# Second expert mixture: half 1's rows scattered by plain transfers, and all shared tiles placed behind the routed ones

## The chip, the cores and the metric

The kernel runs on one core of a Trainium2 chip. The core has a matrix engine (TensorE, called PE in the profile), a vector engine (DVE), a scalar engine (ACT), a general-purpose engine (POOL) and a sequencer for transfers (SP). SP and POOL issue the transfers of this kernel (DMA); 16 DMA engines carry them out. The metric is the device time of one execution in microseconds (us). Faster and slower are told from no change at 0.3%, about 3.7 us here.

## The reference, cut to what matters

Four layers follow each other: attention, a first mixture of experts, a state-space layer, and a second mixture of experts. Only the second mixture is changed:

```python
def _L1_ffn_ref(x, gate_w, gate_b, w1, b1, w3, b3, w2, b2, sw1, sb1, sw3, sb3, sw2, sb2):
    D, H, E, K = 128, 176, 8, 2
    xf = x.reshape(-1, D)                       # 4096 tokens
    scores = jax.nn.softmax(xf @ gate_w.T, axis=-1)
    _, idx = lax.top_k(scores + gate_b, K)      # two experts of eight for each token
    w = jnp.take_along_axis(scores, idx, axis=-1)
    rw = zeros((T, E)).at[arange(T)[:, None], idx].add(w)
    h = silu((einsum('td,edh->teh', xf, w1) + b1) * (einsum('td,edh->teh', xf, w3) + b3))
    oe = einsum('teh,ehd->ted', h, w2) + b2
    y = einsum('te,ted->td', rw, oe)            # the routed experts
    z = _expert(xf, sw1, sb1, sw3, sb3, sw2, sb2)   # the shared expert, for every token
    return (y + z).reshape(shape)
```

## The kernel before

The 4096 tokens are 32 tiles of 128 rows, in two halves of 16 tiles: half 0 (tiles 0 to 15) and half 1 (tiles 16 to 31). In a mixture each half is routed by itself. Each of its tokens is written twice, once for each of its two experts, into a table in device memory (`rows1`, in the code `XG`), at a slot in which the rows of one expert stand together. The table is filled with zeros long before. One write of 128 rows is a **scatter** (`pool_scatter`, line 858): one indirect transfer that POOL issues, with the slots as its index. Half 1 has 32 of them, 16 for the first choice and 16 for the second; between the two passes POOL waits until the first 16 have landed and puts the second weight into the rows (`pool_reweight`, line 852). The argument `op` says whether a scatter adds to what stands in the table (`ALU.add`) or writes over it (`ALU.bypass`).

The **routed tiles** are blocks of 128 rows of that table: 39 for each half (`NH`), 78 in all (`NT`). A routed tile is fetched by SP (line 1074), turned, sent through the expert's two layers by PE, ACT and DVE, weighted, and stored by SP into another table, `out_rows1` (line 1079). The **shared tiles** are the 32 tiles of tokens themselves, fetched by SP from on-chip memory (line 1069). All 110 tiles go through one software pipeline, in the order of the list `sequence`. Each engine walks the list; at step s, SP fetches tile s and stores tile s - 8 (`LAG`), PE turns tile s - 3, and DVE puts out tile s - 6. The fetch of a routed tile waits until its half has been scattered (`placed`), and every fetch waits until the tile four places ahead of it has been turned. SP runs its list in order, so what stands behind a waiting fetch waits as well.

When all routed tiles of a half are stored, POOL **gathers** (line 1131): 32 indirect transfers that add the rows of `out_rows1` to the tokens `X`, 16 for each choice, the second 16 after the first have landed. POOL runs in one order: the scatters of half 1, the gathers of half 0, the gathers of half 1.

The shared tiles of half 0 are added to `X` as they come out (lines 1320 and 1324), after half 0's gathers. Those of half 1 are put into a buffer of their own, `late` (line 1309), and are added to `X` at the very end, four tiles at a time, as soon as half 1's gathers for these tiles have landed (line 1371). SP then writes the output (line 1096).

The stages around the change, in the order of time: the state-space layer (its POOL work is line 1900), the function `dispatch`, which scatters half 0 and routes half 1, and `experts`, called with `inside=False` for the second mixture. The first mixture calls the same `experts` with `inside=True` and no shared tiles. In the names of the profile `m_x_G` is a fetched tile, `m_x_UP`, `m_x_HP` and `m_x_DP` are the matrix engine's outputs, `m_x_YO` a finished tile and `g_X` the tokens.

Of the kernel before, what the change touches and what calls it, by code (L numbers as in the profile page):

```python
# [12 lines left out]
ALU = mybir.AluOpType  # L13
# [5 lines left out]
T = B * S // P  # L19
# [4 lines left out]
HT = T // 2  # L24
NH = 2 * HT + E - 1
NT = 2 * NH
# [898 lines left out]
def experts(nc, tag, signals, d, inside, X, rt, XG, Y, out, n_early, w, gated, ident, ahead=None):  # L925
# [7 lines left out]
    n_shared, scale_col, H = w.n_shared, w.ns, w.H  # L933
# [6 lines left out]
    LAG = 8  # L940
    R = 4 * U

    sequence = [(False, i) for i in range(NH)]
    if n_shared:
        sequence += [(True, i) for i in range(HT, HT + LAG)]
    sequence += [(False, i) for i in range(NH, NT)]
    if n_shared:
        sequence += [(True, i) for i in range(HT)] + [(True, i) for i in range(HT + LAG, T)]
    place_of_shared = {i: j for j, (shared, i) in enumerate(sequence) if shared}

    def stores(v, through):
# [3 lines left out]
    def stores_of(v, end):  # L955

        return sum(1 for j, (shared, i) in enumerate(sequence) if not shared and i < end and j % U == v)
# [27 lines left out]
    with ExitStack() as ctx:  # L985
# [51 lines left out]
        with nc.Block() as block:  # L1037
# [62 lines left out]
            @block.gpsimd  # L1100
            def _(pool):
                if inside:
                    d.pool_scatter(pool, 1, HT // 4, HT, ALU.bypass)
                pool.wait_ge(d.s.sent.sem, d.s.sent.after(0))
                pool.sem_inc(placed, NH)
                for k in range(2):
                    d.pool_reweight(pool, 1, k)
                    d.pool_scatter(pool, k, HT, T, ALU.add)
                pool.wait_ge(d.s.sent.sem, d.s.sent.after(1))
                if inside:  # L1110
                    pool.wait_ge(d.s.tabled.sem, d.s.tabled.after(1))
                pool.sem_inc(placed, NH)
                if out is None:

                    for v in range(U):
                        pool.wait_ge(stored[v], 16 * stores_of(v, NH))
                    for k in range(2):
                        for t in range(n_early):
                            nc.gpsimd.indirect_dma_start(X[:, t * D:(t + 1) * D], None, Y[0:NH * P, :],  # L1119
                                                         bass.IndirectOffsetOnAxis(rt.slot[k][:, t:t + 1], 0),  # L1120
                                                         compute_op=ALU.add).then_inc(early, 16)
                        pool.wait_ge(early, 16 * n_early * (k + 1))
                else:
                    for h in range(2):
                        for v in range(U):
                            pool.wait_ge(stored[v], 16 * stores_of(v, (h + 1) * NH))
                        for k in range(2):
                            if k == 1:
                                pool.wait_ge(joined, 16 * HT * (h + 1))
                            for t in range(h * HT, (h + 1) * HT):  # L1130
                                nc.gpsimd.indirect_dma_start(X[:, t * D:(t + 1) * D], None, Y[0:(h + 1) * NH * P, :],  # L1131
                                                             bass.IndirectOffsetOnAxis(rt.slot[k][:, t:t + 1], 0),
                                                             compute_op=ALU.add).then_inc(got[t % HT // W] if k else joined, 16)
# [70 lines left out]
            def _(act):  # L1204
# [28 lines left out]
                def copy_h(t):  # L1233
                    j, v = t.j, t.v
                    act.wait_ge(h_turned.sem, h_turned.after(j))
                    if t.has(2):
                        act.wait_ge(down_ready.sem, down_ready.after(j - 2))
                    for c, (c0, n) in enumerate(chunks):
                        if n == P:
                            continue  # L1240
                        ins = nc.scalar.activation(hT[v % 2][0:n, c * P:(c + 1) * P], HP[0:n, c * P:(c + 1) * P], ACT.Copy)
                    full = sum(n for _, n in chunks if n == P)
                    ins = nc.scalar.activation(hT[v % 2][:, 0:full], HP[:, 0:full], ACT.Copy)  # L1243
                    ins.then_inc(h_copied.sem, 1)
# [783 lines left out]
def build(nc, a, out):  # L2028
# [6 lines left out]
    with ExitStack() as outer:  # L2035
# [29 lines left out]
        with ExitStack() as ctx:  # L2065
# [39 lines left out]
            attention(nc, rows, early, d0, zeroed, X, shift, scales, ident, w, bias, b_iw, b_o, rope, later_loads, clear)  # L2105

        experts(nc, "m0_x_", tile_signals, d0, True, X, rt, XG0, Y0, None, HT, w0, True, ident, state_rows)
        front.close()
        m = Maker(nc, outer, "m1_")
# [5 lines left out]
        XS1.append(m.sb("XS1", [P, HT, D + 1]))  # L2115
        dispatch(nc, "m1_f_", d1, sent)
        experts(nc, "m1_x_", tile_signals, d1, False, X, rt, XG1, Y1, out, HT, w1, False, ident)

# [72 lines left out]
```

## Time and profile before

| | before |
|---|---|
| median of 3 runs | 1232.14 us (1229.09 to 1233.37) |
| the profiled execution, its own time | 1222.57 us |
| its span, first to last instruction | 1220.7 us |
| PE busy / DVE busy / POOL busy / ACT busy | 982.1 / 946.0 / 835.1 / 741.5 us |
| second mixture's `experts`, from the first fetch | 1014.3 us to the end |

The profiled execution is 9.57 us shorter than the median of the three runs, and its own time is 1.87 us longer than its span. Times inside the span are counted from the first instruction.

### The profile page before, as it was taken

The page shows a single profiled execution, that of the slowest core. Times are in us where ns is not written, and L with a number is a line of the kernel's source. Part 1 is how long each engine was busy: PE and PEld are TensorE (multiplying, and loading weights), DVE is VectorE, ACT ScalarE, POOL GpSimd, SP SyncE. Part 2 cuts the span into 40 slices and gives each one's busy share as a digit, 9 for nine tenths or more (in the row PEclk, how much of TensorE's full clock was granted, in tenths as well). Part 3 has the DMA queues.
Part 4 walks back from the last instruction along what each step waited for, and adds up shares of the span by engine and source line. Part 5 has one row for each costly group of instructions (what it writes and reads, how often), then busy time and mean ns, then how long its engine had stood idle before and what let it go on. Part 6 is the DMA issues. An engine that isn't in the chain of part 4 may idle for free. (4 is left out here: it accounts for less than half of the span.)

```text
span 1220.7 us, 17047 instructions
## 1 busy us (share of the span) xinstructions
PE 982.1 (80%) x4202; PEld 596.9 (49%) x4202; DVE 946.0 (77%) x2295; ACT 741.5 (61%) x1656; POOL 835.1 (68%) x604
## 2 busy tenths in 40 slices
PE   5888868289999977788989988898857736999970
PEld 3666756268888842333333433342413224777750
DVE  6999999753333337799999999999999965777760
ACT  4867747165555557967686776667833215777740
POOL 3333339647527646788999988796949967767676
PEclk9999879589999988998999889999968867999995
DMA  9996002226525425253545353534335315756543
GB/s 271 158 156 179 1 8 20 35 50 92 83 69 92 86 37 125 95 156 124 164 146 173 128 164 102 174 122 138 125 102 151 107 41 90 123 103 122 106 94 65
DMA packets 140032, 133.50 MB, mean 109 GB/s; under 512 B 14578, under 2 KB 121186, under 8 KB 139810
## 3 DMA queue, kind: packets, MB, share of 16 engines
q1 hardware_dynamic: 107106, 115.55, 35.1%
q0 software_dynamic: 32832, 16.86, 12.3%
q8 instruction: 39, 0.64, 0.2%
q14 instruction: 55, 0.45, 0.1%
HBM read 98.66 MB, written 31.60 MB: 107 GB/s over the span
## 5 line engine op out<-in xcount | busy, mean ns | idle before, releaser
L1900 POOL TENSOR_TENSOR ss_HC<-ss_Hs,ss_Cb 128x512 f32<-128x512 f32 x256 | 330.3, 1460 | 75.0 <-DVE ss_Hs L1952 56.3
L1625 PE MATMUL ss_Y<-ss_HC,g_ident 128*128 128x512 f32 x512 | 269.3, 657 | 49.4 <-POOL ss_HC L1900 46.2
L1952 DVE TENSOR_TENSOR_SCAN ss_Hs<-ss_dA,ss_dBu 128x512 f32<-128x512 f32 x256 | 296.8, 1199 | 8.0 <-ACT ss_dA L1801 8.0
L1801 ACT ACTIVATE ss_dA<-ss_delta,g_A 128x510 f32<-128x510 f32 x256 | 168.9, 712 | 94.2 <-DVE ss_Hs L1952 94.0
L858 POOL DMA_INDIRECT rows<-m_XS,g_slot x128 | 178.8, 1397 | 60.3 <-issue 33.6
L1625 PEld LDWEIGHTS ss_Y<-ss_HC,g_ident 128*128 128x128 f32 x512 | 97.3, 205 | 203.1 <-POOL ss_HC L1900 131.6
L1151 PE MATMUL m_x_UP<-g_m_w,m_x_gT 128*128 (+1 forms) x532 | 192.4, 468 | 0.0
L1944 DVE TENSOR_TENSOR ss_dBu<-ss_duP,ss_Bb 128x512 f32<-128x512 f32 x256 | 163.0, 683 | 1.5 <-ACT ss_duP L1781 1.5
L1171 PEld LDWEIGHTS m_x_DP<-g_m_w,m_x_hT 128*128 128x128 f32 x908 | 121.8, 191 | 62.2 <-issue 34.5
L1171 PE MATMUL m_x_DP<-g_m_w,m_x_hT 128*128 (+1 forms) x908 | 140.8, 285 | 2.3 <-ACT m_x_hT L1243 2.3
L1243 ACT ACTIVATE m_x_hT<-m_x_HP 128x256 f32<-128x256 f32 (+1 forms) x188 | 80.4, 428 | 87.2 <-PE m_x_HP L1161 85.5
L1292 DVE SCALAR_TENSOR_TENSOR m_x_hid<-m_x_UP,m_x_G,m_x_sg 128x352 f32<-128x352 f32 x78 | 45.5, 583 | 110.3 <-ACT m_x_sg L1225 110.3
L1131 POOL DMA_INDIRECT g_X<-out_rows,g_slot x64 | 99.6, 1556 | 37.5 <-issue 18.3
L520 POOL TENSOR_TENSOR at_RP<-at_RP,a_rope 128x1024 f32<-128x1024 f32 x16 | 39.5, 2468 | 88.9 <-ACT at_RP L357 88.9
L1151 PEld LDWEIGHTS m_x_UP<-g_m_w,m_x_gT 128*128 128x128 f32 x532 | 87.8, 193 | 18.1 <-issue 1.7
L1299 DVE TENSOR_TENSOR m_x_sg<-m_x_UP,g_m_b 128x352 f32<-128x352 f32 x110 | 57.6, 524 | 32.5 <-PE m_x_UP L1151 32.2
L1161 PE MATMUL m_x_HP<-g_ident,m_x_hid 128*128 128x128 f32 x454 | 80.4, 273 | 2.5 <-DVE m_x_hid L1292 2.4
L1119 POOL DMA_INDIRECT g_X<-out_rows,g_slot x32 | 49.5, 1546 | 44.9 <-DMA out_rows<-m_x_YO 33.7
L1590 PE MATMUL ss_Q<-ss_xpad,ss_w_conv 128*128 128x512 f32 x128 | 60.6, 619 | 7.8 <-ACT ss_xpad L1730 7.8
L1142 PE MATMUL m_x_TP<-g_ident,m_x_G 128*128 128x128 f32 x188 | 52.3, 278 | 16.2 <-DMA m_x_G<-rows 15.0
L1225 ACT ACTIVATE m_x_sg<-m_x_UP 128x352 f32<-128x352 f32 x78 | 36.2, 464 | 39.9 <-PE m_x_UP L1151 39.9
L1161 PEld LDWEIGHTS m_x_HP<-g_ident,m_x_hid 128*128 128x128 f32 x454 | 55.9, 142 | 4.0 <-DVE m_x_hid L1292 2.6
(284 smaller groups left out, 1746.5 us busy)
## 6 DMA issues: line engine op xcount, KB each, us to landing
ss_Bb<-bc_rows SPq DMA_DIRECT2D x64, 512.0 KB, 4.6
ss_Cb<-bc_rows SPq DMA_DIRECT2D x64, 512.0 KB, 3.8
rows<-g_Z SPq DMA_DIRECT2D x2, 5031.0 KB, 53.4
m_x_G<-rows SPq DMA_DIRECT2D x156, 64.5 KB
out_rows<-m_x_YO SPq DMA_DIRECT2D x156, 64.0 KB
g_m_w<-in_w_up SPq DMA_DIRECT2D x1, 2816.0 KB, 11.3
g_m_b<-in_b SPq DMA_DIRECT2D x1, 2160.0 KB, 11.5
g_X<-in_x SPq DMA_DIRECT2D x4, 512.0 KB, 6.1
```

Of the source, the lines that this page charges most:

```text
L858: self.nc.gpsimd.indirect_dma_start(self.XG, bass.IndirectOffsetOnAxis(self.rt.slot[k][:, t:t + 1], 0), self.row(t), None, compute_op=op). ...
L1131: nc.gpsimd.indirect_dma_start(X[:, t * D:(t + 1) * D], None, Y[0:(h + 1) * NH * P, :], bass.IndirectOffsetOnAxis(rt.slot[k][:, t:t + 1], ...
L1151: ins = nc.tensor.matmul(UP[v % 2][:, at:at + n], gT[v % 2][:], w.w[:, ds(e + c, n)], start=True, stop=True)
L1161: ins = nc.tensor.transpose(HP[0:n, c * P:(c + 1) * P], hid[v % 2][:, c0:c0 + n], ident[:])
L1171: ins = nc.tensor.matmul(DP[v % 2][:, 0:D], hT[v % 2][0:n, c * P:(c + 1) * P], w.w[0:n, ds(e + WU + c * D, D)], start=c == 0, stop=c == NC ...
L1243: ins = nc.scalar.activation(hT[v % 2][:, 0:full], HP[:, 0:full], ACT.Copy)
L1590: ins = nc.tensor.matmul(dst, w_conv[:, h, k, :], xpad[:, h, :, k:k + S], start=k == 0, stop=k == K)
L1625: ins = nc.tensor.matmul(Yp[:, h, :], ident[:], HC[(c * N + n) % NHC][:, h, :], start=False, stop=n == N - 1)
L1801: nc.scalar.activation(dA[n % NA][:, h, :, 1:S], seqs(delta[v][:, h, :])[:, :, 1:S], ACT.Exp, scale=A[:, h, n:n + 1]).then_inc(dA_ready.se ...
L1900: nc.gpsimd.tensor_tensor(HC[(c * N + n) % NHC][:, h, :], Hs[n % 4][:, h, :], Cb[g % 2][:, n % 2, :], ALU.mult).then_inc(hc_ready.sem, 1)
L1944: v_.tensor_tensor(dBu[:, h, :], duP[:, h, :], Bb[g % 2][:, n % 2, :], ALU.mult).then_inc(dBu_ready.sem, 1)
L1952: v_.tensor_tensor_scan(Hs[n % 4][:, h, :], dA[n % NA][:, h, :, :].rearrange("p s t -> p (s t)"), dBu[:, h, :], 0.0, ALU.mult, ALU.add).th ...
```

## The change

The two changes touch the second mixture only.

```diff
@@ in experts()
-    sequence = [(False, i) for i in range(NH)]
+    sequence = [(False, i) for i in range(NT)]
     if n_shared:
-        sequence += [(True, i) for i in range(HT, HT + LAG)]
-    sequence += [(False, i) for i in range(NH, NT)]
-    if n_shared:
-        sequence += [(True, i) for i in range(HT)] + [(True, i) for i in range(HT + LAG, T)]
+        sequence += [(True, i) for i in range(HT, T)] + [(True, i) for i in range(HT)]
     place_of_shared = {i: j for j, (shared, i) in enumerate(sequence) if shared}
@@ in the work of POOL
                 for k in range(2):
                     d.pool_reweight(pool, 1, k)
-                    d.pool_scatter(pool, k, HT, T, ALU.add)
+                    d.pool_scatter(pool, k, HT, T, ALU.add if inside else ALU.bypass)
```

The list was: 39 routed tiles of half 0, 8 shared tiles of half 1, 39 routed tiles of half 1, 16 shared tiles of half 0, 8 shared tiles of half 1. It becomes: 39 routed tiles of half 0, 39 of half 1, 16 shared tiles of half 1, 16 of half 0. The 32 scatters of half 1 write instead of adding; in the first mixture (`inside`) they add as before. SP, PE, ACT and POOL issue as many rows of instructions as before; on DVE the same work falls into two rows more.

On SP, at the last fetches of half 0's routed tiles (`m1_x_G` are the four fetch buffers, `rows1` the routed table, `m1_XS1` half 1's tokens, `out_rows1` the table of results). Before:

```order
L1074 DMA m1_x_G2<-rows1 128x129
L1079 DMA out_rows1<-m1_x_YO2 128x128
L1069 DMA m1_x_G3<-m1_XS1 128x128
L1079 DMA out_rows1<-m1_x_YO3 128x128
L1069 DMA m1_x_G0<-m1_XS1 128x128
```

The same place after:

```order
L1071 DMA m1_x_G2<-rows1 128x129
L1076 DMA out_rows1<-m1_x_YO2 128x128
L1071 DMA m1_x_G3<-rows1 128x129
L1076 DMA out_rows1<-m1_x_YO3 128x128
L1071 DMA m1_x_G0<-rows1 128x129
```

The first row is the last fetch of half 0 (tile 38) in both. Behind it stood eight fetches of shared tiles, between which the last eight tiles of half 0 are stored; now the fetches of half 1's routed tiles 39 to 46 stand between these stores, and the first of them waits for all of half 1's scatters. (All line numbers above 947 are three lower after the change.)

At the end of SP's list before, where `x16` and `x24` are fetches with nothing between them and `out` is the kernel's output:

```order
L1069 DMA m_x_G<-m_XS 128x128
L1079 DMA out_rows<-m_x_YO 128x128
L1069 DMA m_x_G<-m_XS 128x128 x16
L1096 DMA out<-g_X 128x4x128 x8
L1037 UNCONDITIONAL_BRANCH
```

And after:

```order
L1066 DMA m_x_G<-m_XS 128x128
L1076 DMA out_rows<-m_x_YO 128x128
L1066 DMA m_x_G<-m_XS 128x128 x24
L1093 DMA out<-g_X 128x4x128 x8
L1034 UNCONDITIONAL_BRANCH
```

The second row is the store of the last routed tile. 16 fetches of shared tiles stood behind it, and 24 do now: that store moved ahead by eight tiles.

## Rows read from the trace of the kernel before

**Rows 1.** Busy us of each engine in two stretches; PEclk is the granted clock.
```profile
1180.00:1200.00 20.00, 2.40 (x16) 1.74 (x16) 2.33 (x6) 1.02 (x4) 15.38 (x11) 0.61 0.32 46
1200.00:1221.00 21.00, 0.00 (x0) 0.00 (x0) 2.08 (x3) 0.00 (x0) 12.58 (x8) 0.50 0.37 66
```

**Rows 2.** End of the chain that ended last: start, length, what.
```profile
1213.18 3.32 DMA g_X<-out_rows,g_slot
...
1216.52 0.69 DVE g_X L1371
```

**Rows 3.** POOL in order of time: half 0's and half 1's gathers, first and last.
```profile
1083.81 1.55 POOL L1131 DMA_INDIRECT g_X<-out_rows,g_slot  x1 [6.11 <-DMA out_rows<-m_x_YO]
...
1143.41 1.54 POOL L1131 DMA_INDIRECT g_X<-out_rows,g_slot  x1 [0.30 <-issue]
1153.76 1.54 POOL L1131 DMA_INDIRECT g_X<-out_rows,g_slot  x1 [8.81 <-DMA out_rows<-m_x_YO]
...
1213.18 1.54 POOL L1131 DMA_INDIRECT g_X<-out_rows,g_slot  x1 [0.30 <-issue]
```

**Rows 4.** SP in order of time: fetches (L1074, L1069) and stores (L1079).
```profile
1014.27 10.12 SPq L1074 DMA_DIRECT2D m_x_G<-rows  x9
...
1070.30 0.50 SPq L1069 DMA_DIRECT2D m_x_G<-m_XS  x1
...
1081.18 0.59 SPq L1079 DMA_DIRECT2D out_rows<-m_x_YO  x1
1082.13 11.82 SPq L1074 DMA_DIRECT2D m_x_G<-rows  x9
...
1151.25 0.59 SPq L1079 DMA_DIRECT2D out_rows<-m_x_YO  x1
```

**Rows 5.** POOL in order of time: half 1's scatters, first and last of each 16.
```profile
1015.34 1.59 POOL L858 DMA_INDIRECT rows<-m_XS,g_slot  x1 [0.52 <-POOL m_XS L852]
...
1043.24 1.55 POOL L858 DMA_INDIRECT rows<-m_XS,g_slot  x1 [0.30 <-issue]
...
1048.22 1.56 POOL L858 DMA_INDIRECT rows<-m_XS,g_slot  x1 [0.50 <-POOL m_XS L852]
...
1076.15 1.55 POOL L858 DMA_INDIRECT rows<-m_XS,g_slot  x1 [0.30 <-issue]
```

**Rows 6.** POOL in order of time: plain scatters, first mixture (12) and dispatch (1, then 16).
```profile
232.70 0.99 POOL L858 DMA_INDIRECT rows<-m_XS,g_slot  x1 [3.52 <-POOLq L222]
...
246.73 0.96 POOL L858 DMA_INDIRECT rows<-m_XS,g_slot  x1 [0.30 <-issue]
...
988.52 0.99 POOL L858 DMA_INDIRECT rows<-m_XS,g_slot  x1 [0.30 <-issue]
...
991.71 0.98 POOL L858 DMA_INDIRECT rows<-m_XS,g_slot  x1 [0.52 <-POOL m_XS L852]
...
1010.77 0.95 POOL L858 DMA_INDIRECT rows<-m_XS,g_slot  x1 [0.30 <-issue]
```

**Rows 7.** DVE in order of time: first shared tile put out; half 1's first routed tile.
```profile
1081.37 0.28 DVE L1309 TENSOR_TENSOR m_x_late<-m_x_DP,g_m_b 128x128 f32<-128x128 f32 x1
...
1092.82 0.28 DVE L1326 TENSOR_TENSOR m_x_YO<-m_x_DP,g_m_b 128x128 f32<-128x128 f32 x1
```

**Rows 8.** Stretches: PE, PEld, DVE, ACT, POOL busy (instructions), PEclk, DMA share, GB/s.
```profile
232.70:247.70 15.00, 5.53 (x33) 5.16 (x34) 10.79 (x61) 3.54 (x5) 11.64 (x12) 0.56 0.15 49
...
1048.20:1078.00 29.80, 29.80 (x181) 21.36 (x180) 21.49 (x61) 23.71 (x98) 24.91 (x16) 1.00 0.77 123
```

**Rows 9.** DVE in order of time, beside the plain scatters of the first mixture.
```profile
239.87 2.39 DVE L705 TENSOR_SCALAR m_XS<-g_X,m_d_mv,m_d_sc 128x128 f32<-128x128 f32 x9
```

**Rows 10.** PE in order of time: the first layer's pair of matmuls, at start and later.
```profile
1017.96 1.42 PE L1151 MATMUL m_x_UP<-g_m_w,m_x_gT 128*128 x2
...
1066.33 0.76 PE L1151 MATMUL m_x_UP<-g_m_w,m_x_gT 128*128 x2
```

## The prediction

> **What bounds the kernel now.** I read the end first. After 1180 us PE has 2.40 us of work left, while POOL stays at work to the end [rows 1], and the chain that ended last runs back from the last addition of late tiles to POOL's last gather [rows 2]. So the end hangs on POOL's list, and the next view is POOL in order of time [rows 3]. Half 1's gathers begin at 1153.76 and the last begins at 1213.18, 59.42 us later; from there to the span's end at 1220.7 are 7.52 us of landing, one addition and the last output. In front of each half's gathers POOL stands idle: 6.11 us ahead of 1083.81 and 8.81 us ahead of 1153.76, both times for a store of routed tiles. The stores answer to that [rows 4]: half 0's last store is issued at 1081.18, 2.63 us ahead of the first gather of half 0, and half 1's last at 1151.25, 2.51 us ahead of the first gather of half 1. Between these two idle times half 0's gathers run without a break; the last of them begins at 1143.41, takes 1.54 us, and the next could begin 0.30 us behind it, at 1145.25. The kernel's end is therefore the later of two things plus a fixed 66.9 us (59.42 + 7.52): POOL free from half 0 (1145.25), or half 1's routed tiles stored (1153.76). Now the second decides, by 8.51 us.
>
> **The change, part by part.**
>
> *The eight shared tiles leave their place between the halves.* What they take there is read on DVE, which puts out one tile per step: the first shared tile at 1081.37, half 1's first routed tile at 1092.82 [rows 7]. That is 11.45 us for eight tiles, 1.43 us each. Without them half 1's last store falls to 1151.25 - 11.45 = 1139.80, and its gathers could start 2.51 us later, at 1142.31. POOL is not free then but at 1145.25, so of the 11.45 us only 8.51 reach the end, and 2.94 us are lost to a POOL that is now never idle between its gathers.
>
> *Half 0 must not move for this.* Its gathers start behind its last store. The eight steps in which its last eight tiles are finished were filled with fetches of shared tiles and are now filled with routed ones. A routed tile costs at most 1.54 us (half 1's first output at 1092.82 to its last store at 1151.25 are 58.43 us for 38 steps [rows 4, 7]) where a shared one costs 1.43; eight times the difference is 0.9 us, the most by which half 0's last store slips. The least is nothing, since the matrix work for these last tiles stands ahead of nearly all of the new steps. I take nothing: the old store rate up to 1081.18 was already that of routed tiles.
>
> *The scatters have to be done earlier.* The fetch of the first shared tile stood at 1070.30; it is now the fetch of half 1's first routed tile, which waits for all 32 scatters. Before, that fetch stood at 1082.13 [rows 4], and the last scatter was issued at 1076.15 [rows 5]: at the old pace it would be late. An adding scatter comes every 1.86 us ((1043.24 - 1015.34)/15 [rows 5]). Plain ones stand in two places [rows 6]: every 1.28 us in the first mixture (14.03 us for 11 steps) and every 1.27 us in dispatch (19.06 us for 15). From the last scatter of the first choice to the first of the second, landing and new weights included, a plain pass takes 3.19 us (988.52 to 991.71), an adding one beside these experts 4.98 us (1043.24 to 1048.22). So half 1's plain scatters should run from 1015.34 to 1034.4 (15 x 1.27), again from 1037.6 or 1039.4 to 1056.6 or 1058.5, and have landed after no more than the same pause again, between 1059.8 and 1063.4. The fetch that needs them stands at 1070.30: at least 6.9 us to spare, and SP never waits.
>
> Is a plain scatter this cheap beside experts? In the stretch of the twelve plain ones DVE is busy 10.79 of 15 us, in that of the adding ones 21.49 of 29.8, both 72% [rows 8]; the first stretch has a DMA share of 0.15 and the second 0.77, so only the load on the transfers differs, and part of that load are the adding scatters themselves. In the middle of the twelve, DVE runs nine float operations from on-chip memory to on-chip memory [rows 9], and the pace of 1.28 us holds. The Trainium skill, "SBUF — State Buffer", section "SBUF: two separate sides", says that POOL cannot write its descriptors while DVE is in certain two-port modes, so that a transfer from POOL seems held up by DVE. By that rule the scatters could take any longer pace; by the rows they keep theirs, and the trace does not show the rule at work here. If it did, it would be the first rival below.
>
> *The tail.* PE has the same 110 tiles without a gap and ends as before, a few us after 1180 [rows 1]. The last to come out are now half 0's shared tiles, whose additions and output fall near 1184, some 28 us ahead of the new end; before, half 1's last late tiles came out there. The additions of late tiles still wait for half 1's gathers alone. All this is hidden, and costs one for one only if it came more than those 28 us later.
>
> **Sum.** 8.51 us less: a span of 1212.2 us, and 1214.1 us for the profiled execution's own time (1222.57). The three runs stand higher, at a median of 1232.14, 9.57 us above the profiled execution; I see no reason why the change should touch that difference and take it over: 1232.14 - 8.5 = 1223.6 us.
>
> **The rivals.**
>
> *The scatters land late, and it gets no faster or slower.* The place is SP's fetch of tile 39. If it waits, the stores of half 0's tiles 31 to 38 wait behind it in SP's list, and with them half 0's gathers; before, these stores were ahead of the waiting fetch. Call L the time at which all scatters have landed. Up to 1070.3 nothing is lost. Beyond that PE runs dry, and the eighth fetch from there on, with half 0's last store behind it, comes about 9 us after L (nine fetches from a standing start take 10.12 us [rows 4]). At the pace of adding scatters L would be at most 1076.15 + 4.98 = 1081.1; half 0's last store then falls near 1090 in place of 1081.18, its gathers end 8.9 us later, and half 1's begin at 1154.2 in place of 1153.76. PE also starts again at the low clock: the first pair of matmuls took 1.42 us at the start of this stage and 0.76 later [rows 10]; two such tiles are some 1.3 us. That makes 0.4 to 1.7 us more than before, 1232.5 to 1233.8 us. The gain is gone from L = 1080 on, and it is slower by 0.3% from about L = 1083.5, a pace of 1.94 us per scatter; at 2.1 us it would be some 1240. For it speaks the DMA share of 0.77; against it that POOL's own time per plain scatter is 0.95 to 0.99 us in every place where it stands. By that rule of the Trainium skill on DVE and POOL, if it held here, this is what would come. Chance 0.10, one half of it within 0.3% and one half above.
>
> *Half 0's last stores slip.* They now share SP and the DMA engines with fetches from device memory, and each us of slip moves every gather and the end by 1 us. At 1 to 5 us the gain is 7.5 to 3.5 us: 1224.6 to 1228.6. Against it: the scatters are over by then, so the engines carry less than before. Chance 0.09.
>
> *The whole 11.45 us.* Then half 0's gathers would have to end 2.94 us earlier than now, 1220.7 us. They run at a fixed pace behind a store that does not move; only a quicker landing between the two choices could help. Chance 0.03.
>
> **How the numbers follow.** My forecast, half 1's gathers right behind half 0's, holds 0.78. From the three runs (1229.09 to 1233.37) less 8.5, and less 7.6 with the slip of 0.9 us, its own range is 1220.6 to 1225.8. The whole range goes to 1230 at the top, which takes in the slipped stores but not the late scatters, and to 1216 at the bottom, because the difference of 9.57 us between the profiled execution and the runs is not explained and may come out smaller in other runs (without it, 1214.1). Faster by over 0.3% (3.7 us): the forecast, the third rival, and most of the second, 0.87. Within 0.3%: 0.08. Slower: 0.05.
>
> **What would show it.** In the profile of the changed kernel: 32 scatters at a pace near 1.27 us with the last issued near 1057; the first fetch of half 1 near 1070 and PE without a gap there; half 0's first gather still near 1083.8; half 1's last store near 1140; no idle time of POOL between the two halves' gathers, whose second half starts near 1145.3; the end of PE near 1183. A gap on PE near 1072 with half 0's first gather later than 1084 would show the first rival, a first gather later without that gap the second. I am wrong altogether if plain scatters cost more than 1.5 us each beside the experts.

## The result, and the profile after

The changed kernel takes 1256.99 us (median of four runs, 1254.87 to 1260.11) where the kernel before takes 1230.73 (1229.09 to 1233.37): 1.0223 times as long, 95% interval 1.0198 to 1.0248. It was forecast to be 8.5 us faster and is 26 us slower.

POOL in order of time in the changed kernel: half 1's plain scatters (L858, first and last of each 16), then the gathers of half 0 and of half 1 (L1128), first and last.

```profile
1024.06 0.98 POOL L858 DMA_INDIRECT rows<-m_XS,g_slot  x1 [0.53 <-POOL m_XS L852]
...
1043.03 0.96 POOL L858 DMA_INDIRECT rows<-m_XS,g_slot  x1 [0.30 <-issue]
1046.21 0.98 POOL L858 DMA_INDIRECT rows<-m_XS,g_slot  x1 [0.52 <-POOL m_XS L852]
...
1065.16 0.95 POOL L858 DMA_INDIRECT rows<-m_XS,g_slot  x1 [0.30 <-issue]
1128.19 1.59 POOL L1128 DMA_INDIRECT g_X<-out_rows,g_slot  x1 [62.08 <-DMA out_rows<-m_x_YO]
...
1187.77 1.54 POOL L1128 DMA_INDIRECT g_X<-out_rows,g_slot  x1 [0.30 <-issue]
1189.62 1.54 POOL L1128 DMA_INDIRECT g_X<-out_rows,g_slot  x1 [0.30 <-issue]
...
1250.75 1.54 POOL L1128 DMA_INDIRECT g_X<-out_rows,g_slot  x1 [0.30 <-issue]
```

Against [rows 3] and [rows 5] two things have come true. The scatters take 0.96 us each and follow one another every 1.26 us, and the last is issued 42.2 us after the stage's first fetch (1065.16 - 1022.99), where it was 61.9 us before (1076.15 - 1014.27). And half 1's gathers follow half 0's without a pause: 0.30 us in front of 1189.62 in place of 8.81. But half 0's own gathers begin 105.2 us after the first fetch (1128.19 - 1022.99), where it was 69.5 us (1083.81 - 1014.27), and POOL stands idle for 62.08 us ahead of them. That is 35.7 us, the whole loss and more. SP's list shows where they went.

SP in order of time, the fetches (L1071) and stores (L1076) of the first 50 us of the stage; the last row is half 1's last store.

```profile
1022.99 12.57 SPq L1071 DMA_DIRECT2D m_x_G<-rows  x9
1035.61 0.45 SPq L1076 DMA_DIRECT2D out_rows<-m_x_YO  x1
1047.83 0.32 SPq L1071 DMA_DIRECT2D m_x_G<-rows  x1
1048.20 0.43 SPq L1076 DMA_DIRECT2D out_rows<-m_x_YO  x1
1056.40 0.32 SPq L1071 DMA_DIRECT2D m_x_G<-rows  x1
...
1070.59 0.32 SPq L1071 DMA_DIRECT2D m_x_G<-rows  x1
...
1184.12 0.59 SPq L1076 DMA_DIRECT2D out_rows<-m_x_YO  x1
```

After nine fetches and one store SP gets on by one tile at 1047.83, one at 1056.40, one at 1070.59, and from then on by one every 1.5 to 2.7 us. This is not the wait for the scatters, which stands some 30 tiles further on. The tiles themselves stand still, and only while the scatters run. The next rows are busy time by stretch (PE, PEld, DVE, ACT, POOL with instructions, PEclk, DMA share, GB/s): the two stretches of the scatters, and the one behind them.

```profile
1024.00:1044.00 20.00, 9.00 (x30) 5.01 (x30) 3.66 (x9) 4.78 (x17) 15.36 (x16) 0.67 0.31 83
1044.00:1070.00 26.00, 6.06 (x18) 3.99 (x18) 2.84 (x8) 2.74 (x12) 15.54 (x17) 0.57 0.18 54
1080.00:1100.00 20.00, 20.00 (x122) 14.48 (x122) 14.13 (x41) 16.16 (x69) 0.00 (x0) 1.00 0.36 93
```

Before, PE was busy all the time beside the adding scatters [rows 8]. Now it is busy for 6.06 of 26 us, DVE for 2.84 and ACT for 2.74, and the DMA engines have a share of 0.18 where it was 0.77. POOL alone spends most of the stretch at work, on its scatters (15.54). The granted clock, 1.00 beside the adding scatters [rows 8], is 0.57 in this stretch in which PE stands idle for 20 of 26 us, most of it thus at 1.2 GHz; it is back at 1.00 (2.4 GHz) in the last row. What they wait for is in the list of waits from 1022 to 1072 us (us in total, times, longest; four of its rows). An engine that has finished an instruction raises a counter, its signal, and another engine that needs the result waits for that counter.

```profile
ACT m_x_hT L1240 <- remote: 31.8, 3, 13.0
PE m_x_DP L1168 <- ACT m_x_hT L1240: 27.7, 3, 11.1
DVE m_x_YO L1323 <- remote: 17.2, 3, 7.6
DVE m_x_sg L1296 <- remote: 9.3, 3, 5.6
```

```profile
1034.42 0.38 PE L1158 MATMUL m_x_HP<-g_ident,m_x_hid 128*128 128x128 f32 x2
1035.29 0.30 PE L1139 MATMUL m_x_TP<-g_ident,m_x_G 128*128 128x128 f32 x1 [0.49 <-issue]
...
1046.86 0.38 ACT L1240 ACTIVATE m_x_hT<-m_x_HP 128x256 f32<-128x256 f32 x1 [11.43 <-remote]
1046.93 0.29 DVE L1323 TENSOR_TENSOR m_x_YO<-m_x_DP,g_m_b 128x128 f32<-128x128 f32 x1 [7.57 <-remote]
```

ACT's copy `m_x_hT` needs PE's two turns of `m_x_HP`, which end at 1034.80, and PE goes on with the next tile at 1035.29. ACT starts 12 us later. The trace also records when a signal arrives, for some of the instructions. End of the instruction, arrival of its signal:

```
PE  L1168 m_x_DP   1032.12   1032.13
PE  L1158 m_x_HP   1034.80   1046.84
PE  L1139 m_x_TP   1035.59   1046.88
PE  L1148 m_x_UP   1036.37   1049.67
ACT L1240 m_x_hT   1047.25   1047.26
DVE L1323 m_x_YO   1047.23   1047.24
PE  L1158 m_x_HP   1057.59   1069.57
PE  L1139 m_x_TP   1057.80   1069.61
```

PE's signals arrive up to 13.3 us late (that of 1036.37, for which DVE's L1296 of the same tile starts only at 1049.79), some together 0.04 us apart, while the recorded ones of ACT and DVE in this stage arrive at once. The delay builds up: the scatters begin at 1024.06, and the signal of 1032.12 is still on time; the next ones recorded are 2.3 us late at 1034.76, 5.3 at 1038.34 and 12 at 1046.8. In the profile of before, 173 recorded signals of PE between 1014 and 1085 us are 0.015 us late at most.

### The profile page after: what moved, and what is told of

Read it like the earlier page. It is cut to its first block and busy times, and to the rows that moved or that the text cites. A ratio compares the mean times of both kernels' runs of the same rounds, so it can differ in the third digit from the quotient of the medians.

```text
span 1258.2 us, 17047 instructions
## 1 busy us (share of the span) xinstructions
PE 996.2 (79%) x4202; PEld 608.1 (48%) x4202; DVE 944.5 (75%) x2295; ACT 741.3 (59%) x1656; POOL 816.9 (65%) x604
## 5 line engine op out<-in xcount | busy, mean ns | idle before, releaser
L858 POOL DMA_INDIRECT rows<-m_XS,g_slot x128 | 159.1, 1243 | 59.5 <-issue 33.5
L1148 PE MATMUL m_x_UP<-g_m_w,m_x_gT 128*128 (+1 forms) x532 | 195.3, 474 | 0.0
L1168 PEld LDWEIGHTS m_x_DP<-g_m_w,m_x_hT 128*128 128x128 f32 x908 | 124.9, 195 | 92.4 <-issue 66.3
L1168 PE MATMUL m_x_DP<-g_m_w,m_x_hT 128*128 (+1 forms) x908 | 143.4, 288 | 30.9 <-ACT m_x_hT L1240 30.0
L1128 POOL DMA_INDIRECT g_X<-out_rows,g_slot x64 | 100.1, 1565 | 86.0 <-DMA out_rows<-m_x_YO 62.4
L1296 DVE TENSOR_TENSOR m_x_sg<-m_x_UP,g_m_b 128x352 f32<-128x352 f32 x110 | 57.6, 524 | 50.0 <-PE m_x_UP L1148 29.6
```

The costliest lines, as they stand in the source:

```text
L858: self.nc.gpsimd.indirect_dma_start(self.XG, bass.IndirectOffsetOnAxis(self.rt.slot[k][:, t:t + 1], 0), self.row(t), None, compute_op=op). ...
L1148: ins = nc.tensor.matmul(UP[v % 2][:, at:at + n], gT[v % 2][:], w.w[:, ds(e + c, n)], start=True, stop=True)
L1168: ins = nc.tensor.matmul(DP[v % 2][:, 0:D], hT[v % 2][0:n, c * P:(c + 1) * P], w.w[0:n, ds(e + WU + c * D, D)], start=c == 0, stop=c == NC ...
```

## The experiments

The theory after this, called H in the expectations (held signals): while plain scatters are under way on POOL, PE's signals are held up, and the experts stand still. The rivals are the order of the tiles (O), and that the profile shows an accident (N). The edits below are cut to the lines that matter. "Stage to gather" below is the time from the stage's first fetch to half 0's first gather: 69.5 us in the first profile of before, 105.2 in the changed kernel.

**The kernel before once more.** No edit.

> The kernel before, unchanged, for a second profile. Its first profiled execution took 1222.57 us where its timed ones take 1229 to 1233, and showed no wait that the profile puts down to an unknown source; the changed kernel's profile shows such waits not only beside half 1's plain scatters but also, 4.7 and 1.7 us long, in the dispatch, which the change does not touch. Theory H (held signals): while plain scatters are under way TensorE's signals reach ScalarE and VectorE late, and the timed runs of before have a few us of that in the two places where before has plain scatters too. H expects a profile near 1230 with some such waits beside the plain scatters at 232 to 248 or 985 to 1014, or, where the time is near 1222 again, none. Rival N (the profile of the changed kernel was a disturbed execution and the waits are an accident of it): no such waits whatever the time.

1230.21 us, span 1228.4. One row of its waits, and POOL's first gather of each half:

```profile
ACT m_d_xT L731 <- remote: 3.2, 1, 3.2
```

```profile
1091.39 1.55 POOL L1131 DMA_INDIRECT g_X<-out_rows,g_slot  x1 [6.74 <-DMA out_rows<-m_x_YO]
...
1161.71 1.54 POOL L1131 DMA_INDIRECT g_X<-out_rows,g_slot  x1 [9.07 <-DMA out_rows<-m_x_YO]
```

The stage is as in the first profile (69.8 us to the gather, 9.07 us idle between the halves). But in the first mixture's dispatch two signals of PE, of instructions that end at 248.23 and 249.92, come 2.38 and 2.25 us late, beside or just behind the plain scatters there; the remote wait of ACT is the one for the first of them. In the second mixture's dispatch two of PE are 0.7 us late and some of DVE up to 0.9. So the first profile, from which [rows 6] and [rows 8] were read, was an execution without a late signal, and plain scatters do hold signals in other executions of the same kernel. N falls. Against this profile the changed kernel's span is 29.8 us longer: stage to gather +35.4, the start of the stage +1.4, the idle time between the halves -8.8, the gathers and the tail +1.8.

**The order alone.**

```diff
-                    d.pool_scatter(pool, k, HT, T, ALU.add if inside else ALU.bypass)
+                    d.pool_scatter(pool, k, HT, T, ALU.add)
```

> The new order of tiles alone; half 1's scatters stay adding ones. Theory H (the plain kind of scatter holds up TensorE's signals, the order is innocent): experts run at their old pace to about 1070, SP waits for the last adding scatter some 10 us with six stores behind it, half 0's gathers start about 10 us later than in the kernel before, POOL has no idle time between the gathers of the two halves: 1230 to 1240 us where before is 1231. Theory O (the order is to blame: SP stands at a routed fetch with half 0's stores behind it): most of the 26 us remains, 1250 us or more.

1229.35 us, 0.9985 of before (0.9964 to 1.0006): no difference, and just below the range that H gave. No remote wait in the experts. POOL's first gather of each half, and two neighbouring rows of SP:

```profile
1099.19 1.55 POOL L1128 DMA_INDIRECT g_X<-out_rows,g_slot  x1 [15.19 <-DMA out_rows<-m_x_YO]
...
1160.45 1.54 POOL L1128 DMA_INDIRECT g_X<-out_rows,g_slot  x1 [0.30 <-issue]
```

```profile
1075.89 0.43 SPq L1076 DMA_DIRECT2D out_rows<-m_x_YO  x1
1085.88 0.32 SPq L1071 DMA_DIRECT2D m_x_G<-rows  x1
```

The 9.07 us between the halves are gone, and half 0's gathers come 8.9 us later in the stage (78.7 us), because SP stands at the fetch of tile 39 (1085.88) with stores behind it. O falls; this is what the first rival of the prediction described, and its 8.9 us, but without the change of scatter.

**The plain scatters alone**, on the kernel before.

```diff
-                    d.pool_scatter(pool, k, HT, T, ALU.add)
+                    d.pool_scatter(pool, k, HT, T, ALU.add if inside else ALU.bypass)
```

> The plain scatters alone; the order of tiles is that of before. Theory H: the experts stand still beside the scatters as in the changed kernel, half 0's first gather comes some 30 us or more later than 1083.8 plus what the start of the stage has shifted, and with eight shared tiles still between the halves the end is set by half 1's last store: 1255 to 1270 us. Theory O: the scatters land before they are needed and the old order keeps SP free: 1228 to 1233 us, as before. Waits put down to an unknown source: H, beside the scatters, 10 us each; O, none.

1261.76 us, 1.025 (1.0221 to 1.0278). Stage to gather 103.3 us, and the idle time between the halves is there again (8.93 us).

```profile
ACT m_x_hT L1243 <- remote: 28.2, 3, 12.1
DVE m_x_YO L1326 <- remote: 14.3, 3, 6.2
```

```profile
1122.62 1.59 POOL L1131 DMA_INDIRECT g_X<-out_rows,g_slot  x1 [59.95 <-DMA out_rows<-m_x_YO]
...
1192.87 1.61 POOL L1131 DMA_INDIRECT g_X<-out_rows,g_slot  x1 [8.93 <-DMA out_rows<-m_x_YO]
```

The plain scatters are the cause; the order only decides whether 9 us are given back behind them.

**Four at a time.**

```diff
+                        for q in range(0, HT, 4):
+                            d.pool_scatter(pool, k, HT + q, HT + q + 4, ALU.bypass)
+                            pool.wait_ge(d.s.sent.sem, d.s.sent.after(1, 16 * (k * HT + q + 4)))
```

> The changed kernel, but GpSimd waits for the landing after every four plain scatters of half 1, so that no more than four are under way. Theory H with the kind alone as its cause: the signals are held as long as any are under way, so the experts stand still about as long, 1253 to 1262 us. Theory Q (it is the number of scatters under way, or queued, that holds them): most of the stall goes, since the landing of four leaves gaps; the scatters take some 8 times 2 us longer, last landing near 1080, 1222 to 1235 us. Theory O: as the changed kernel or later, since the scatters end later.

1240.01 us, 1.0061 (1.004 to 1.0081). Stage to gather 85.2 us; no signal of PE is more than 2.9 us late. POOL's pause behind a batch, and the waits:

```profile
1030.08 0.96 POOL L858 DMA_INDIRECT rows<-m_XS,g_slot  x1 [1.79 <-DMA rows<-m_XS,g_slot]
```

```profile
ACT m_x_hT L1245 <- remote: 8.1, 3, 3.1
```

More than half of the stall is gone, which points to theory Q, but the time lies outside the ranges of both theories. It does not tell yet whether the number under way or POOL's pause did it.

**What in a plain scatter does it.** Four kernels: pauses on POOL without waiting for a landing, a quarter of the bytes, a quarter of the rows, and the counter-test, no plain scatter in the whole program.

```diff
 # pauses: behind each plain scatter of half 1
+                            nc.gpsimd.memset(spare[:], 0.0).then_inc(d.s.reweighted.sem, 1)   # 128x640
+                            pool.wait_ge(d.s.reweighted.sem, d.s.reweighted.after(1, k * HT + k + 1 + t - HT + 1))
 # a quarter of the bytes: rows of 32 columns, to a table of their own
+        nc.gpsimd.indirect_dma_start(narrow, bass.IndirectOffsetOnAxis(rt.slot[k][:, t:t + 1], 0), d.row(t)[:, 0:32], None)
 # a quarter of the rows
+        nc.gpsimd.indirect_dma_start(d.XG, bass.IndirectOffsetOnAxis(rt.slot[k][0:32, t:t + 1], 0), d.row(t)[0:32], None)
 # no plain scatter, on the kernel before, at all four places
-                d.pool_scatter(pool, 1, 0, HT, ALU.bypass)
+                d.pool_scatter(pool, 1, 0, HT, ALU.add)
```

> The changed kernel with a memset of about 0.6 us on GpSimd, awaited, behind each plain scatter of half 1, so that they follow one another every 1.9 us or a little more, the adding ones' pace; no landing is awaited. Theory P (the plain scatters hold the signals while GpSimd writes their descriptors one after the other, and any pause lets the signals through): each signal is at most some 2 us late, the stall falls from 36 us to 10 or less, and the scatters land near 1086 to 1090, after the fetch that needs them, so 1230 to 1245 us. Theory F (a plain scatter under way holds them, whoever works meanwhile; the pause of the run with four at a time helped because nothing was under way in it): one or two are always under way, the stall is as long as the scatters, 60 us instead of 44, and the time 1255 us or more.

1229.87 us, 0.9998 (0.9979 to 1.0016). No remote wait and no late signal of PE in the experts; the 62 us of scatters end as late as adding ones, and stage to gather is 77.3 us for SP's wait. POOL:

```profile
1028.12 0.96 POOL L858 DMA_INDIRECT rows<-m_XS,g_slot  x1 [0.28 <-POOL m_x_spare L1111]
1029.09 0.65 POOL L1111 MEMSET m_x_spare<- 128x640 f32 x1
```

> The changed kernel, but half 1's plain scatters move only the first 32 of the 129 columns, to a table of their own (half 1's routed rows then hold zeros: the result leaves out what its tokens get from the routed experts). As many rows and descriptors, a quarter of the bytes. Theory P: the signals are as late as with whole rows, 1250 to 1262 us. Theory B (it is the bytes that are written, or read from SBUF, that stand in the signals' way): the stall falls to a third or less, 1218 to 1232 us.

1258.34 us, 1.0236 (1.0206 to 1.0266); stage to gather 104.0 us.

> The changed kernel, but each plain scatter of half 1 moves only the first 32 of its 128 rows, whole (three quarters of half 1's routed rows are left out of the result). A quarter of the rows, of the descriptors and of the bytes, the same number of scatters. Theory P with the descriptors as its cause, and theory B: the stall falls to a third or less, 1215 to 1232 us. Theory I (it is the issuing of a plain scatter, whatever it holds): if GpSimd takes as long for each, the stall stays, 1250 to 1262 us. The duration of the issue on GpSimd, 0.96 us with 128 rows, tells how much of it is rows.

1259.98 us, 1.0241 (1.0214 to 1.0268); stage to gather 105.0 us. Issue and wait with a quarter of the bytes, then with a quarter of the rows:

```profile
1021.11 0.96 POOL L1110 DMA_INDIRECT narrow_rows<-m_XS,g_slot  x1 [0.30 <-issue]
```

```profile
ACT m_x_hT L1246 <- remote: 28.8, 3, 11.5
```

```profile
1024.15 0.87 POOL L1109 DMA_INDIRECT rows<-m_XS,g_slot  x1 [0.30 <-issue]
```

```profile
ACT m_x_hT L1245 <- remote: 29.1, 3, 19.7
```

> The kernel before with every scatter an adding one: also the 12 of the first mixture near 232 us, and those in and ahead of the second mixture's dispatch. The memory that they add to is zeroed at the start. Theory H: the waits put down to an unknown source (one of 3.2 us in the second profile of before) are gone from the whole profile, and no signal of TensorE is late; the time is the sum of that gain (some 8 us, the distance of the two profiles of before) and of scatters that are 0.59 us longer, 7 us where twelve are on the path and up to 11 us in the dispatch: 1225 to 1242 us. Rival S (the signals are late beside any scatter, and the plain ones of half 1 only meet a stage that minds it more): the late signals stay.

1247.03 us, 1.0148 (1.0115 to 1.0181): slower than expected, since the stage's first fetch comes at 1036.41 in place of 1021.6; the adding scatters ahead of it are on the path. But its profile has no remote wait at all and no late signal of PE, in the first mixture and in dispatch neither.

So it is neither the bytes nor the rows: a quarter of either leaves the stall whole, and POOL takes 0.87 us to issue 32 rows where it takes 0.96 for 128. It is not a scatter under way either: a landing takes 1.8 us from the end of the issue (the wait shown for four at a time), so in the spaced run, with one issue of 0.96 us every 1.9 us, one is nearly always under way, and nothing is held. What the stall goes with is POOL's issuing plain scatters one after the other, 0.30 us apart. Theories B and F fall, I stands (and P, read as the issue and not the descriptors).

**How long the pause must be.** The same memset behind every second scatter only; with 256 columns; with 32 columns; and no memset, but every second scatter of half 1 an adding one.

```diff
+                        for t in range(HT, T, 2):              # pairs
+                            d.pool_scatter(pool, k, t, t + 2, ALU.bypass)
-        spare = m.sb("spare", [P, 640])
+        spare = m.sb("spare", [P, 256])                        # short;  [P, 32]: tiny
+                        d.pool_scatter(pool, k, t, t + 1, ALU.add if inside or t % 2 else ALU.bypass)   # alternate
```

> As the spaced run (a memset of 0.65 us, awaited, that makes GpSimd's pause between two plain scatters 0.92 us in place of 0.30), but the pause stands behind every second scatter only. Theory P (signals wait while GpSimd issues plain scatters back to back, and any longer pause lets them through): a signal is at most about 2.5 us late, the experts lose some us in all, the scatters land near 1077, in time for their fetch, so half 0's gathers start near where before has them and half 1's follow with no idle time: 1219 to 1228 us. Theory E (the pause must stand behind each scatter, since the hold-up builds up over any two in a row): the stall of the changed kernel comes back by half, 1238 to 1250 us.

1224.74 us, 0.9965 (0.9949 to 0.9982); stage to gather 73.0 us, signals at most 0.63 us late.

> As the spaced run, with a memset of 256 columns in place of 640, some 0.3 us: one plain scatter every 1.55 to 1.6 us. Theory P: no signal late by more than 1 us, the scatters land near 1077, SP hardly waits, half 0's gathers start within 2 us of where the second profile of before has them (1091), and the 9 us of idle time between the halves' gathers are gone: 1219 to 1225 us. Theory E': a pause of 0.6 us is too short to let signals through: the stall comes back in part, 1230 to 1250 us.

1222.24 us, 0.9949 (0.9933 to 0.9966), the lowest median of all, though not clear of the pairs above and the alternating run below. Its pause, its first gather of each half, and PE beside the scatters:

```profile
1022.61 0.96 POOL L858 DMA_INDIRECT rows<-m_XS,g_slot  x1 [0.28 <-POOL m_x_spare L1111]
1023.57 0.33 POOL L1111 MEMSET m_x_spare<- 128x256 f32 x1
...
1090.47 1.60 POOL L1135 DMA_INDIRECT g_X<-out_rows,g_slot  x1 [16.59 <-DMA out_rows<-m_x_YO]
...
1152.00 1.54 POOL L1135 DMA_INDIRECT g_X<-out_rows,g_slot  x1 [0.30 <-issue]
```

```profile
1044.00:1070.00 26.00, 25.41 (x155) 18.20 (x154) 18.24 (x52) 20.27 (x86) 19.25 (x32) 1.00 0.51 126
```

Stage to gather is 70.5 us, PE is busy 25.41 of 26 us, and half 1's gathers follow with 0.30 us of idle time: what was forecast of the change. Four signals of PE are over 0.3 us late, the latest 0.75.

> As the spaced run, with a memset of 32 columns, 0.1 us: one plain scatter every 1.35 us, hardly slower than the changed kernel's 1.26. Theory P with the length of the pause as its measure: the pause grows from 0.30 to about 0.40 us, and the stall is nearly that of the changed kernel, 1245 to 1260 us. Theory M (what helps is that GpSimd does other work, or waits for a signal, between two plain scatters, however short): no stall, scatters landed near 1070, 1218 to 1224 us.

1250.98 us, 1.0166 (1.0139 to 1.0194); stage to gather 96.1 us.

```profile
1028.52 0.97 POOL L858 DMA_INDIRECT rows<-m_XS,g_slot  x1 [0.28 <-issue]
1029.49 0.14 POOL L1111 MEMSET m_x_spare<- 128x32 f32 x1
```

```profile
ACT m_x_hT L1247 <- remote: 23.4, 6, 5.0
```

> The changed kernel with every second of half 1's scatters an adding one, no memset: 16 plain ones, each followed by an adding one of 1.55 us. Theory P or M (only plain ones back to back hold the signals, and an adding one lets them through): no stall or one of a few us, one scatter every 1.56 us in the mean, landed near 1077: 1219 to 1226 us. Theory K (each plain scatter holds the signals by itself): half of the changed kernel's stall, 1238 to 1248 us.

1223.65 us, 0.9957 (0.994 to 0.9973); stage to gather 71.3 us, signals at most 0.49 us late.

M falls: doing something else for 0.14 us is little help, the length counts. From issue to issue the pause is 0.42 us in the tiny one (0.14 + 0.28) and most of the stall is there; it is 0.61 us in the short one (0.33 + 0.28), and the stall is gone. An adding scatter in between does as well as a pause. The number under way does not decide: counted from the start of the issue to the end of the last packet, it is 1.48 in the mean in the changed kernel, 1.44 in the short-pause run and 1.73 with the adding scatters of before. Nor does the pace over the whole pass: four at a time, the last scatter is issued 54.9 us after the first fetch, later than with the short pause (52.6), and signals are held all the same, in the runs of four. What stays untold is kind against pace from one scatter to the next: plain ones hold signals at 1.26 and 1.38 us from start to start and not at 1.57, and adding ones never followed one another faster than every 1.85 us.

**What is left.** Two questions: does before itself lose time to its own plain scatters, and what is the order worth alone? The first two kernels make every second one of the other plain scatters an adding one, in the kernel before and in the short-pause version; the third is the short-pause version with the old order.

```diff
-                                              self.row(t), None, compute_op=op).then_inc(self.s.sent.sem, 16)
+                                              self.row(t), None, compute_op=ALU.add if t % 2 else op).then_inc(self.s.sent.sem, 16)
```

> The kernel before, with every second one of its own plain scatters (those of the first mixture's stage near 232 us and of the second mixture's dispatch) turned into an adding one, so that no two plain ones follow each other; half 1's stay adding ones. Theory H: the late signals there go, worth up to the 8 us by which the timed runs of before lie above its first profile; the scatters there last 0.3 us longer in the mean, 3.6 us for the twelve of the first mixture and 5 us in the dispatch, where GpSimd has some 5 us to spare: 1224 to 1231 us, no wait put down to an unknown source. Rival D (the distance between that first profile and the timed runs has another cause): 1231 to 1237 us.

1235.96 us, 1.0056 (1.0038 to 1.0074).

> The short-pause version (new order, half 1's scatters plain with a pause of some 0.6 us) with the same edit of the other plain scatters: nowhere do two plain scatters follow each other without a longer pause. Theory H: the gains add up, 1216 to 1223 us. Rival D: the longer scatters cost and nothing is won, 1223 to 1230 us.

1229.32 us, 1.0022 (1.0001 to 1.0043), 7 us more than the short-pause version.

> The short-pause version with the order of tiles of before: half 1's scatters plain, with the pause, eight shared tiles between the halves' routed ones. If the order is worth what the prediction said (8.5 us off the end, since GpSimd stands idle between the halves' gathers), this one is 7 to 9 us slower than the short-pause version, at 1227 to 1233 us, with some 9 us of idle time ahead of half 1's gathers; if it is the quicker scatters that bring the gain and the order brings nothing, 1221 to 1224 us.

1229.45 us, 1.001 (0.9988 to 1.0031). Half 1's first gather:

```profile
1160.72 1.54 POOL L1138 DMA_INDIRECT g_X<-out_rows,g_slot  x1 [9.11 <-DMA out_rows<-m_x_YO]
```

In the first two no remote wait is left, as H says, but the time is Rival D's: ahead of the stage the longer scatters are on the path (its first fetch at 1029.76 in place of 1021.6), and the 2 to 4 us that a signal is late there are worth less than that. The third shows what the order brings: 7.2 us (1229.45 - 1222.24), with 9.11 us of idle time ahead of half 1's gathers in place of 0.30.

## Why the prediction was wrong

**The eight shared tiles** were sized rightly. 8.51 us were to go from the end, and 8.8 us of idle time went in the changed kernel and in the run of the order alone; where nothing else moves, 7.2 us of the time go (the last run against the short pause). The bound on it, that POOL then goes from half 0's gathers to half 1's without a pause, holds in the runs of the new order.

**The scatters have to be done earlier**: right in its own terms. Their pace was 1.26 us, and all had landed long before the fetch that needs them. The condition named at the end, more than 1.5 us per scatter, did not come about, and the prediction fell all the same.

**Half 0 must not move for this** is the step that failed. Its slip was put at 0 to 0.9 us and was 35.7. The step asked what the new fetches on SP cost half 0's stores, and not what the new scatters do to half 0's tiles. The passage "Is a plain scatter this cheap beside experts?" asked only one way round: whether the experts slow the scatters down. The Trainium skill's rule that was weighed there ("SBUF — State Buffer", section "SBUF: two separate sides") says that POOL can't write its descriptors while DVE is in certain two-port modes; the trace after shows nothing of it, 0.95 to 0.98 us per scatter. DVE has little work there, but beside a busy DVE, in the short-pause run (18.24 of 26 us), 31 of the 32 take 0.96 to 0.99 us too. What happened was the reverse, POOL holding up the others. The rows used for it could not show that: in the first mixture's stretch [rows 8] PE was busy for 5.53 of 15 us and DVE worked by itself, so hardly a signal of PE was waited for, and that execution was one without late signals. The second profile of before has two there.

**The second rival** named the right place, half 0's last stores, at 1 to 5 us and a chance of 0.09, and was argued down with "the engines carry less than before". The DMA share did fall, to 0.18, and the stores slipped all the same: it was not a matter of the load on the transfers. **The first rival** is what the order does with adding scatters, and its 8.9 us are what the run of the order alone measured; its time, 1232.5 to 1233.8, was 3.2 to 4.5 us too high (1229.35).

**The difference between the profile and the runs** was taken over unexplained. The second profile of before (span 1228.4) takes most of it away: its first copy of weights (L852) is 2.4 us later, before any plain scatter runs (170.5 in place of 168.1), and some 3 us come where signals are late in the first mixture. For a sum this made no difference, but looking for it in a second profile would have shown the late signals.

## What to carry to other kernels

When a transfer is made cheaper to issue, ask not only whether the others slow it down but what its issuing does to the others, and read that from a stretch in which they hang on each other's signals at every step. Here GpSimd's plain indirect transfers belong apart, with 0.6 us between them or an adding one in each gap: the change with that pause is 0.5% faster than the kernel before, and without it 2.2% slower. And a wait put down to nobody on two engines at once, with the engines idle but for the one that issues, is a sign to look at when signals arrive, not at how long work takes.

## What the runs showed of the hardware

Plain indirect transfers issued by GpSimd 0.30 us apart hold up the signals of TensorE, by up to 13.3 us in the changed kernel (with a quarter of the rows one wait of ScalarE lasts 19.7 us). They come out singly or in groups 0.04 us apart, also while the scatters go on (1049.67, 1053.28, 1055.4 and 1060.38 in the changed kernel), the last of them 3.5 us after the end of the last issue. A short series holds less: 2.9 us at most with four in a row, 0.63 with two. Stage to gather by pause: 105.2 us at 0.30, 96.1 at 0.42, 70.5 at 0.61; with adding transfers at 0.30 us, which take 1.55 us to issue, 69.5 to 69.8 in the two profiles of before.

The profile's end of a matmul does not show it. The Trainium skill, "Perfetto Trace Analysis", section "Tensor Engine Instruction (MATMUL, LD_WEIGHTS)", says that this end is estimated, and that the signal is pushed only after PSUM has acknowledged the last write, outside the window shown; the trace agrees that the two are apart: 0.015 us at most in the first profile of before, up to 13.3 us here. So whether the matmul's last write or only its signal is late can't be read from PE's rows. VectorE's rows say a little more. In the run with a quarter of the rows, beside dispatch's plain scatters, its L820 ends at 1015.71, its signal is recorded at 1017.42, and the next instruction, which waits for it, is this one:

```profile
1017.44 0.17 DVE L821 TENSOR_TENSOR m_d_first<-m_d_end,m_d_ct 128x8 f32<-128x8 f32 x1 [1.73 <-remote]
```

There the work was over and the signal 1.7 us late.

What in the chip is shared by GpSimd's issuing and by the signals stays open. So does one thing about the record: in the first profile of before, which has no late signal, 4 of 177 records of PE's signals between 1014 and 1085 us are missing; in later profiles it can be half of them, with late signals (e.g. the four at a time, 31 of 112) and almost without (the short pause, 80 of 159). Whether recording has a part in the hold-up no run here shows.
